# Attention scores from two float32r halves in 64 rows, with one scratch tensor that holds every operand row

## The reference, cut to what matters

```
h = layernorm(x)
qkv = h @ w_attn.T + b_attn + 0.5 * (h @ la_attn.T @ lb_attn.T)
q, k, v = split(qkv)                       # 16 heads of 16 channels each
att = einsum('bhqd,bhkd->bhqk', q, k) * 0.25
att = where(causal, att, -inf);  att = softmax(att)
y = einsum('bhqk,bhkd->bhqd', att, v)
```

## Time and profile before

| | |
|---|---|
| median of three runs | 1599.78 us |
| the three runs | 1598.96, 1599.78, 1600.34 us |
| span of the profiled execution, first to last instruction | 1598.6 us |
| TensorE (PE) busy | 1482.5 us, 93% |
| ScalarE (ACT) busy | 1270.6 us, 79% |
| VectorE (DVE) busy | 343.7 us, 22% |
| GpSimd (POOL) busy | 338.5 us, 21% |
| DMA over the span | 65.65 MB, 41 GB/s on average |
| mean granted TensorE clock | 0.957 of full |

### The profile page before, as it was taken

How to read it: one execution, slowest core, us unless ns; L and a number is a source line. 1 busy time by engine, 2 the same in 40 slices (tenths; PEclk the granted TensorE clock), 3 DMA queues, 4 the chain that set the end, 5 groups by cost and what they waited for, 6 DMA issues and landing times. The chain is left out here.

```text
span 1598.6 us, 27053 instructions
## 1 busy us (share of the span) xinstructions
PE 1482.5 (93%) x8838; PEld 582.0 (36%) x8838; DVE 343.7 (22%) x903; ACT 1270.6 (79%) x1584; POOL 338.5 (21%) x940
## 2 busy tenths in 40 slices
PE   6799599999989999998999999899999887998995
PEld 3355222222222222222222222222222276887784
DVE  3488200000000000000000000000000075569746
ACT  2477399999979999997999999799999836455644
POOL 1532100000120000012000001100001137445754
PEclk7699799999999999998999999899999988999998
DMA  5144430000130000012001002200000040011001
GB/s 145 40 151 155 115 97 21 21 21 21 28 82 1 21 21 21 21 47 62 1 21 21 21 21 54 55 1 1 1 1 5 23 158 1 1 54 53 1 1 53
DMA packets 71175, 65.65 MB, mean 41 GB/s; under 512 B 14080, under 2 KB 66688, under 8 KB 71040
## 3 DMA queue, kind: packets, MB, share of 16 engines
q1 hardware_dynamic: 67504, 61.18, 13.3%
q10 hardware_dynamic: 3536, 2.72, 0.6%
HBM read 42.51 MB, written 21.36 MB: 40 GB/s over the span
## 5 line engine op out<-in xcount | busy, mean ns | idle before, releaser
L718 ACT ACTIVATE probs<-S 128x1024 f32<-128x1024 f32 (+3 forms) x1152 | 1015.8, 964 | 90.1 <-PE S L750 79.0
L750 PE MATMUL S<-q_op,k_op 99*128 99x512 bf16 (+3 forms) x2304 | 568.8, 368 | 33.8 <-DMA q_op<-shift 15.3
L768 PE MATMUL O<-probs,vg 128*32 128x512 f32 (+3 forms) x4608 | 577.1, 574 | 0.5 <-POOL probs L694 0.5
L750 PEld LDWEIGHTS S<-q_op,k_op 99*128 99x128 bf16 x2304 | 174.4, 98 | 611.0 <-ACT probs L718 461.0
L694 POOL TENSOR_SCALAR_AFFINE_SELECT probs<-probs 128x256 f32<-128x256 f32 x256 | 102.9, 408 | 981.9 <-ACT probs L718 978.5
L730 DVE COPY acc<-O 128x512 f32 x16 | 11.1, 692 | 820.7 <-PE O L768 820.7
L918 PE MATMUL psC<-wfT,yTC 128*128 128x256 f32 x768 | 175.6, 387 | 8.6 <-ACT yTC L979 6.2
L768 PEld LDWEIGHTS O<-probs,vg 128*32 128x32 f32 x4608 | 91.4, 108 | 225.9 <-issue 206.7
L918 PEld LDWEIGHTS psC<-wfT,yTC 128*128 128x128 f32 x768 | 146.8, 194 | 30.6 <-ACT yTC L979 7.8
L966 ACT ACTIVATE yC<-uC,nmrC,rstdC 128x256 f32<-128x256 f32 x128 | 66.4, 590 | 57.2 <-POOL nmrC L90 57.1
L973 ACT COPY yTC<-psC 128x1024 f32<-128x1024 f32 x32 | 31.6, 1007 | 56.1 <-PE psC L911 56.1
(11 more groups left out here) (100 smaller groups left out, 799.5 us busy)
## 6 DMA issues: line engine op xcount, KB each, us to landing
qk_parts<-parts SPq DMA_DIRECT2D x32, 384.0 KB, 2.6
q_op<-qk_parts SPq DMA_DIRECT2D x192, 64.0 KB
k_op<-qk_parts SPq DMA_DIRECT2D x192, 64.0 KB
acc<-in_L_attn_x SPq DMA_DIRECT2D x8, 512.0 KB, 4.1
acc_sums<-acc SPq DMA_DIRECT2D x16, 256.0 KB, 2.1
xC<-in_L_attn_x SPq DMA_DIRECT2D x8, 512.0 KB, 4.8
acc<-acc_sums SPq DMA_DIRECT2D x4, 1024.0 KB, 5.9
out<-uC SPq DMA_DIRECT2D x8, 512.0 KB, 3.0
```

Source lines behind the costliest of these rows:

```text
L718: nc.scalar.activation(probs[:, pair % NP, :, 0:TT - q0], S[:, pair % NS, :, 0:TT - q0], ACT.Exp, scale=SCALE).then_inc(exp_ok, 1)
L750: last = nc.tensor.matmul(S[:, pair % NS, a, 0:TT - q0], k_op[0:ROWS, h, kb * P:(kb + 1) * P], q_op[0:ROWS, h, j * TT + q0:(j + 1) * TT], ...
L768: last = nc.tensor.matmul(O[h * STRIP:(h + 1) * STRIP, o % 2, q0:TT], vg[:, kb, h, :], probs[:, (2 * b + h // 2) % NP, h % 2, 0:TT - q0], ...
```

## The change

Each q or k value is split into two float32 halves of 12 significant bits (a mask of the low 12 bits, and a subtraction), and all four products of halves are formed: 4 times 16 channels are 64 rows. The scores of one head take 64 of TensorE's rows, and the two heads of a pair lie beside each other, one in rows 0 to 63 and one in rows 64 to 127, in float32r. Two scratch tensors become one, `rows`, with 64 rows for each head, written out in full: each half is stored twice, so that each operand tile is loaded by a single DMA. Where a guard has run, it overwrites the last rows (the product of the two low halves, 16 rows) with shift, zero and one rows; here it doesn't run. In the core of the diff:

```diff
-PARTS = 3
-Q_PART = (0, 1, 2, 0, 1, 0)
-K_PART = (0, 0, 0, 1, 1, 2)
-SHIFT0 = D * len(Q_PART)
-ROWS = SHIFT0 + PARTS
+PARTS = 2
+HIGH_BITS = -4096
+HALF = P // 2
+Q_PART = (0, 1, 0, 1)
+K_PART = (0, 0, 1, 1)
+SHIFT0 = HALF - D
+PAIRS = HG // 2
# prepare_weights: the zero rows, their memset and their store are gone
-                sp.wait_ge(shift_zero, 1)
-                sp.dma_start(d["shift"].rearrange("s h t -> (s h t)").rearrange("(p n) -> p n", p=P), no_shift[:, :]).then_inc(shift_stored, 16)
-                sp.wait_ge(shift_stored, 16)
-                nc.gpsimd.memset(no_shift[:, :], 0.0).then_inc(shift_zero, 1)
# project
-        parts = sb("parts", [P, 4, PARTS, TT], BF16)
+        parts = sb("parts", [P, 4, PARTS, TT], F32)
+        COPIES = 16 * len(Q_PART)
-                        dst = d["qk_parts"][m // 2, :, (m % 2) * P:(m % 2 + 1) * P, bass.ds(n * TT, TT)]
-                        sp.dma_start(dst.rearrange("s p t -> p s t"), parts[:, m, :, :]).then_inc(stored[m], 16)
+                        for r, part in enumerate((Q_PART, K_PART)[m // 2]):
+                            dst = d["rows"][m // 2, (m % 2) * (H // 2):(m % 2 + 1) * (H // 2), r * D:(r + 1) * D, bass.ds(n * TT, TT)]
+                            sp.dma_start(dst, parts[:, m, part, :]).then_inc(stored[m], 16)
# ScalarE
-                        act.wait_ge(stored[m], (n + 1) * 16)
-                        nc.scalar.activation(sq[:, m, :], psQ[:, m, :], ACT.Square, bias=g["bqk"][:, m:m + 1]).then_inc(sq_ok, 1)
-                        nc.scalar.activation(parts[:, m, 0, :], psQ[:, m, :], ACT.Identity,
-                                             bias=g["bqk"][:, m:m + 1]).then_inc(full_ok, 1)
+                        nc.scalar.activation(sq[:, m, :], psQ[:, m, :], ACT.Square, bias=g["bqk"][:, m:m + 1]).then_inc(full_ok, 1)
# GpSimd
-                    nc.gpsimd.memset(g["k_op"][SHIFT0:ROWS, :, :], 1.0).then_inc(ones_ok, 1)
-                    pool.wait_ge(ones_ok, 2)
# VectorE
-                        nc.vector.tensor_tensor(res[:, s, :], qf[:, s, :], parts[:, m, 0, :], ALU.subtract).then_inc(res_ok, 1)
-                        dve.wait_ge(res_ok, n * 8 + m * 2 + 1)
-                        nc.vector.tensor_copy(parts[:, m, 1, :], res[:, s, :]).then_inc(res_ok, 1)
-                        dve.wait_ge(res_ok, n * 8 + m * 2 + 2)
-                        nc.vector.tensor_tensor(parts[:, m, 2, :], res[:, s, :], parts[:, m, 1, :], ALU.subtract).then_inc(split_ok, 1)
+                        dve.wait_ge(stored[m], (n + 1) * COPIES)
+                        nc.vector.tensor_scalar(parts[:, m, 0, :].bitcast(I32), qf[:, s, :].bitcast(I32), HIGH_BITS, None,
+                                                ALU.bitwise_and).then_inc(high_ok, 1)
+                        dve.wait_ge(high_ok, n * 4 + m + 1)
+                        nc.vector.tensor_tensor(parts[:, m, 1, :], qf[:, s, :], parts[:, m, 0, :], ALU.subtract).then_inc(split_ok, 1)
# the loads of a tile
-def load_parts(eng, d, op, kinds, which, h0, tok, done):
-    for r, part in enumerate(kinds):
-        src = d["qk_parts"][which, part, bass.ds(h0 * D, HG * D), tok].rearrange("(a e) t -> e a t", e=D)
-        eng.dma_start(op[r * D:(r + 1) * D, :, tok], src).then_inc(done, 16)
+def load_rows(eng, d, op, which, g, tok, done):
+    src = d["rows"][which, bass.ds(g * HG, HG), :, tok].rearrange("(p a) r t -> (a r) p t", a=2)
+    eng.dma_start(op[:, :, tok].bitcast(F32), src).then_inc(done, 16)
# attend, SyncE and TensorE
-                    load_parts(sp, d, q_op, Q_PART, 0, i * HG, tok, op_loaded[s])
-                    load_parts(sp, d, k_op, K_PART, 1, i * HG, tok, op_loaded[s])
-                    sp.dma_start(q_op[SHIFT0:ROWS, :, tok], d["shift"][:, bass.ds(i * HG, HG), tok]).then_inc(op_loaded[s], 16)
+                    load_rows(sp, d, q_op, 0, i, tok, op_loaded[s])
+                    load_rows(sp, d, k_op, 1, i, tok, op_loaded[s])
-                            h = 2 * (pair % 2) + a
-                            last = nc.tensor.matmul(S[:, pair % NS, a, 0:TT - q0], k_op[0:ROWS, h, kb * P:(kb + 1) * P],
-                                                    q_op[0:ROWS, h, j * TT + q0:(j + 1) * TT], start=True, stop=True)
+                            mine = slice(a * HALF, (a + 1) * HALF)
+                            last = nc.tensor.matmul(S[:, pair % NS, a, 0:TT - q0], k_op[mine, pair % 2, kb * P:(kb + 1) * P],
+                                                    q_op[mine, pair % 2, j * TT + q0:(j + 1) * TT], start=True, stop=True)
# build
-    d["qk_parts"] = nc.dram_tensor("qk_parts", [2, PARTS, C, T], BF16).ap()
-    d["shift"] = nc.dram_tensor("shift", [PARTS, H, T], BF16).ap()
+    d["rows"] = nc.dram_tensor("qk_rows", [2, H, HALF, T], F32).ap()
# q_op and k_op: [P, HG, T] in BF16 become [P, PAIRS, T] in F32R
```

More of the change, by code:

```diff
@@ L18 @@
 I32 = mybir.dt.int32
+F32R = mybir.dt.float32r
 ALU = mybir.AluOpType
@@ L331, in _ @@
                 for m in range(4):
-                    act.sem_inc(stored[m], 16)
+                    act.sem_inc(stored[m], COPIES)
                 act.sem_inc(full_ok, BANKS)
@@ L506, in guard @@
         neg = sb("neg", [P, P], F32)
-        rest = sb("rest", [P, P], F32)
-        sh = sb("sh", [P, PARTS, P], BF16)
+        sh = sb("sh", [P, PARTS, P], F32)
         S = ctx.enter_context(nc.psum_tensor("SG", [P, 2, KEYS], F32))
@@ L512, in guard @@
         held = sem("heldG")
-        shift_rows = d["shift"].rearrange("s (g a) (b q) -> g (a b) s q", a=HG, q=P)
-        LOADS = len(Q_PART) + len(K_PART)
+        shift_rows = d["rows"][0, :, SHIFT0:SHIFT0 + PARTS, :].rearrange("(g a) s (b q) -> g a b s q", a=HG, q=P)
+        zeros = sb("zeros", [P, H * T // P], F32)
+        ones = sb("ones", [P, H * T // P], F32)
+        fills_ok, filled = sem("fills_ok"), sem("filled")
+        LOADS = 2
         with nc.Block() as block:
@@ L524, in _ @@
                         hold(sp, op_used, i + 1, held)
-                        load_parts(sp, d, q_op, Q_PART, 0, i * HG, slice(0, T), op_loaded)
-                        load_parts(sp, d, k_op, K_PART, 1, i * HG, slice(0, T), op_loaded)
+                        load_rows(sp, d, q_op, 0, i, slice(0, T), op_loaded)
+                        load_rows(sp, d, k_op, 1, i, slice(0, T), op_loaded)
+                    sp.wait_ge(op_loaded, NG * LOADS * 16)
+                    sp.wait_ge(fills_ok, 2)
+                    rest = range(SHIFT0 + PARTS, HALF)
+                    for r in rest:
+                        sp.dma_start(d["rows"][0, :, r, :].rearrange("h (x n) -> h x n", n=H * T // P), zeros[:, :]).then_inc(filled, 16)
+                    for r in range(SHIFT0, SHIFT0 + PARTS):
+                        sp.dma_start(d["rows"][1, :, r, :].rearrange("h (x n) -> h x n", n=H * T // P), ones[:, :]).then_inc(filled, 16)
+                    sp.wait_ge(filled, 16 * (len(rest) + PARTS))
             @block.scalar
@@ L531, in _ @@
                 with act.If(need == 1):
-                    act.sem_inc(sh_stored, 16)
+                    act.sem_inc(sh_stored, 16 * HG)
                     with act.Fori(0, NG) as i:
                         act.wait_ge(sh_ok, i + 1)
-                        act.dma_start(shift_rows[i], sh[:, :, :]).then_inc(sh_stored, 16)
-                    act.wait_ge(sh_stored, 16 * (NG + 1))
+                        for a in range(HG):
+                            act.dma_start(shift_rows[i, a], sh[a * QB:(a + 1) * QB, :, :]).then_inc(sh_stored, 16)
+                    act.wait_ge(sh_stored, 16 * HG * (NG + 1))
             @block.gpsimd
@@ L541, in _ @@
                 with pool.If(need == 1):
+                    nc.gpsimd.memset(zeros[:, :], 0.0).then_inc(fills_ok, 1)
+                    nc.gpsimd.memset(ones[:, :], 1.0).then_inc(fills_ok, 1)
                     nc.gpsimd.memset(ident_b[:, :], 0.0).then_inc(z_ok, 1)
@@ L558, in _ @@
                     with dve.Fori(0, NG) as i:
-                        with dve.Fori(0, HG) as a:
+                        for a in range(HG):
                             for c, (b, k) in enumerate(chunks):
@@ L562, in _ @@
                                 dve.wait_ge(scored, i * STEPS + a * NCH + c + 1)
-                                nc.vector.reduce_max(mx[:, k // KEYS, bass.ds(a * QB + b, 1)], S[:, c % 2, 0:w], AX.X).then_inc(reduced, 1)
+                                nc.vector.reduce_max(mx[:, k // KEYS, a * QB + b:a * QB + b + 1], S[:, c % 2, 0:w], AX.X).then_inc(reduced, 1)
                         dve.wait_ge(reduced, i * STEPS + HG * NCH + 2)
@@ L568, in _ @@
                         dve.wait_ge(reduced, i * STEPS + STEPS + 2)
[L570 to L578, removed]
+                        dve.wait_ge(sh_stored, (i + 1) * (16 * HG))
+                        nc.vector.tensor_scalar(sh[:, 0, :].bitcast(I32), neg[:, :].bitcast(I32), HIGH_BITS, None,
+                                                ALU.bitwise_and).then_inc(chain, 1)
```

(11 more changed lines are left out.)

13 lines of the change are left out of this document (5 added, 8 removed).

## The result

The changed kernel takes 1629.9 us (median of four runs, 1628.7 to 1630.4) against 1599.6 before (median of four runs, too); the ratio is 1.0185 (95% interval 1.0172 to 1.0197). The direction was right, the size was not: 1687 was forecast with a range of 1645 to 1765, and the measured +30 us is a third of the +87. The two large numbers behind it are a loss of 84.8 us up to the first scores, and a gain of 55.3 us in attention that the forecast had at 4.

What follows compares the result with a forecast made beforehand. It took ScalarE to bound attention and TensorE the project stage, which would turn DMA-bound. Profile 1598.6 + 91.6 (to first scores) - 4 (attention) = 1686.2, median 1.2 above: 1687 us, range 1645 to 1765.

Steps and rivals of the forecast that it cites:

- What bounds the kernel: Kernel before: ScalarE's exponentials set attention's 1.96 us block, TensorE could spare little; TensorE bounds the project stage.
- Attention, -4 us: Attention stage: long blocks stay at ScalarE's 1.96 us, only waits at tile and group ends change; -4 us.
- One pass: Attention score products: float32r taken to run in one pass, 0.21 us a pair side by side instead of 0.43.
- Removing slack: Attention's long blocks: less TensorE work there gains nothing, since ScalarE holds the block at 1.96 us.
- Rival 3: Attention: TensorE becomes the bound; +190 us, 1880 in all, or over 2100 in four passes; chance 0.05.
- The stores on 8 engines: Project stage: each store dealt out over the same eight DMA engines, 1.43 us each, 183.2 for 128; chance 0.73.
- Sum to the first scores, +91.6: Project stage to attention's start: DMA-bound at 24.7 us a tile, first scores at 279.3 instead of 187.73; +91.6 us.
- The gap behind the x load, 1 us a tile: Project stage: x load queues behind the previous tile's stores and VectorE waits; 1 us each, 6 in all.
- rival 1: Project stage: stores use sixteen engines, a tile takes 13.0 us, kernel about 1590 us (1583 to 1600); chance 0.11.
- The memset: Before the project stage's first store: without POOL's 13.75 us memset the store comes at about 67.5 instead of 72.28.
- Rival 2: Project stage: the scratch layout slows stores to 15.5 B/ns an engine, +87 us, 1774 in all; chance 0.10.

Runs made afterwards that it cites:

- sixteen-engine version: Changed kernel with q and k channels reordered so each store's outermost DRAM dimension is 16 instead of 8: 1575.7 us, 0.9847 of before.

## Why the prediction was wrong, step by step

- *What bounds the kernel* ("A block takes 1.96 us because of ScalarE"): the step that failed. It rested on exponentials with no idle before them and on a weight load that waits for ScalarE. Both hold with TensorE as the bound: the load's wait of 0.84 us for ScalarE is the same with half the exponential, where ScalarE idles, and costs nothing there, and "no idle" hides 0.06 us an exponential. Halving ScalarE's work left the block at 1.97; halving the weighing took it to ScalarE's real floor, 1.83. The sum 0.97 + 1.00 = 1.97, which the prediction wrote down and set aside, was the bound.
- *Attention, -4 us*: measured -55.3. Of it, 35.0 is the fall of ScalarE's busy time (1015.8 to 980.8), which is read here as waiting hidden in the records (at the same floor bfloat16 has 979.1, side by side, and 981.1, with half the weighing); the rest is idle time between them. One pass, as taken, was right: four products one after another took 1.12 us, 0.28 each, where a float32 product took 0.89. So was side by side: with both heads in the same 64 rows the score phase took 1.13 us, side by side 0.83. "Removing slack" was wrong; the gain ends at ScalarE's floor, 0.14 us a long block.
- *Rival 3, TensorE as the bound*: it was the bound already, and the change moved it away. The rival looked for the loss only.
- *The stores on 8 engines*: right, from the 3 marks of one load. By the Trainium skill's rule ("DMA: Bandwidth & Descriptors", "Why a DMA increments its semaphore by 16 and not by 1") the same low-numbered engines take part each time. The trace agrees that they are the same eight: the share stays near 0.5 however many stores are queued. That they are the low-numbered ones no run here shows.
- *Sum to the first scores, +91.6*: +84.8. A tile took 25.1; the forecast's 24.7 is its total over eight tiles, two of them without an x load, and by its terms a tile with one takes 25.5 (22.9 + 1.6 + 1). The first operand load was issued at 265.1, not 274.0: the first tile's 16 stores, with nothing queued ahead, were issued in 19.3 us (from 67.65), and the last two tiles have no x load to wait for. From there to the first scores took 7.5 us, not 5.3.
- *The gap behind the x load, 1 us a tile*: about right with eight engines (the tile of 25.1 leaves less than 1), where the four stores of m = 0 cover it. With sixteen the cover is half as long, and rival 1 (1590 us) left it out: with attention at the forecast's 1087.3 in place of the 1037.1 measured in the sixteen-engine version, that kernel would have been about 1626, not 1590 (an estimate).
- *The memset*: first store forecast at 67.5, issued at 67.7.
- *Rival 2*, stores slowed by the layout: no. With all engines full (the x load on another queue, the same places in the scratch), 347 GB/s went over 16 engines, 21.7 B/ns each.

## What to carry to other kernels

When two engines both look full, add up the phases of each over one period before naming the bound, and compare the mean length of a record with the spacing: if records can overlap by a quarter, "no idle" proves nothing. A change that takes work off an engine that looked second may then be worth everything down to the other's floor. And look at the outermost dimension of both sides of every store: an order of the same bytes was worth 54 us here. Then look at what a load stands behind in its issuing engine's program: moving one 512 KB load a tile was worth 25 more.

## What the hardware showed that was not expected

TensorE's granted clock fell to 0.50 (1.2 of 2.4 GHz) in stretches of hundreds of us with the engine 100% busy, when score products used 64 rows one after another (three traces; the mean clock of all five executions was 0.681 to 0.869), and was 0.95 to 1.00 in the long stretches of attention in the traces with two of them side by side or with 99 or 128 rows. That is no rule: the kernel before, with 99 rows, had mean clocks of 0.738 and 0.564 in two of its seven executions on one chip, of which no trace is kept. Times of such kernels also differ from run to run (1744 and 1848). What decides when it falls and rises is left open. Four 64-row float32r products a block, two and two side by side, took 0.83 us with the switch to and from the weighing, while ScalarE set the pace; one after another they took 1.13 where the clock was 1.00.
